# Second tile of each image's token product in three passes of rounded parts and rests

## What is computed

```python
p = x.reshape(n, C, NP, PS, NP, PS).transpose(0, 2, 4, 1, 3, 5).reshape(n, NP * NP, D_IN)
tokens = jnp.einsum('npd,hd->nph', p, W) + b
tokens = jnp.concatenate([cls, tokens], axis=1) + pos_embed[None]
...
h = jnp.concatenate([h, txt], axis=1)
h = h + _L0_attn_ref(_layernorm(h, axis=-1), L0_attn_W_qkv, L0_attn_b_qkv)
h = h + _L0_ffn_ref(_layernorm(h, axis=-1), L0_ffn_Wg, ..., L0_ffn_Wsd)
```

## Time and profile before

| | us |
|---|---|
| median of 3 runs | 701.12 |
| lowest, highest | 699.82, 701.9 |
| the profiled execution | 699.24 |
| its span in the trace | 697.4 |
| TensorE busy | 678.6 |
| VectorE busy | 469.4 |
| ScalarE busy | 332.0 |
| GpSimd busy | 201.4 |

### The profile page before, as it was taken

How to read it: one execution, slowest core, us unless ns; L and a number is a source line. 1 busy time by engine, 2 the same in 40 slices (tenths; PEclk the granted TensorE clock), 3 DMA queues, 4 the chain that set the end, 5 groups by cost and what they waited for, 6 DMA issues and landing times.

```text
span 697.4 us, 16667 instructions
## 1 busy us (share of the span) xinstructions
PE 678.6 (97%) x4613; PEld 635.5 (91%) x4614; DVE 469.4 (67%) x1490; ACT 332.0 (48%) x803; POOL 201.4 (29%) x309
## 2 busy tenths in 40 slices
PE   6989999999999999999999999999999999999997
PEld 6879988899988888799999999999999999999997
DVE  2357878888788878765666566666675757576653
ACT  2245555565555666444445343434444434343543
POOL 3022223223223210202323233333333242424240
PEclk9899999999999999999999999999999999999999
DMA  7236434545344321733445454545454545454542
GB/s 232 89 99 210 129 112 148 158 154 152 115 137 141 108 95 63 182 61 63 95 103 108 104 103 106 105 106 104 105 107 102 106 102 107 98 108 97 103 88 56
DMA packets 75188, 79.54 MB, mean 114 GB/s; under 512 B 6505, under 2 KB 67065, under 8 KB 75162
## 3 DMA queue, kind: packets, MB, share of 16 engines
q1 hardware_dynamic: 62538, 65.69, 33.9%
q0 software_dynamic: 11760, 12.31, 11.6%
q10 hardware_dynamic: 864, 1.25, 0.6%
HBM read 51.91 MB, written 19.32 MB: 102 GB/s over the span
## 4 chain that ended last, share of the span: by engine, by line
PE 80%; DVE 10%; issue 4%; ACT 2%; DVEq 1%; POOL 1%; POOLq 0%; ACTq 0%
PE bank L1275 24%; PE bank L1243 12%; PE bank L1292 8%; PE bank L1073 8%; PE bank L1255 8%; PE bank L1061 6%; PE bank L1293 4%; PE bank L1103 3%; PE bank L1217 2%; DVE stats L1454 1%; DVE w_raw L1565 1%; PE bank L1131 1%; PE bank L1088 1%; DVE y_B L1474 1%; DVE h L1490 1%
## 5 line engine op out<-in xcount | busy, mean ns | idle before, releaser
L1740 DVE TENSOR_TENSOR s_inter<-s_gate,bank 128x384 f32<-128x384 f32 (+1 forms) x112 | 60.2, 539 | 73.2 <-PE bank L1275 67.0
L906 ACT ACTIVATE s_gate<-bank 128x384 f32<-128x384 f32 (+1 forms) x112 | 53.5, 478 | 79.1 <-PE bank L1275 79.0
L1292 PE MATMUL bank<-s_dn,s_in_hi 128*128 128x384 f32 (+1 forms) x287 | 88.9, 371 | 0.3 <-DVE s_in_lo L1748 0.2
L727 POOL DMA_INDIRECT result<-y_rows,put_idx x40 | 59.8, 1496 | 57.8 <-DVE y_rows L1727 42.1
L1275 PE MATMUL bank<-all_hiA,s_hi 128*128 (+4 forms) x210 | 73.9, 352 | 0.6 <-DVE s_inter L1740 0.6
L1293 PE MATMUL bank<-s_dn,s_in_lo 128*128 128x192 f32 (+1 forms) x287 | 72.9, 254 | 0.0
L1073 PE MATMUL bank<-w_tok,patches 128*128 128x192 f32 x360 | 68.4, 343 | 4.2 <-DMA patches<-xp 4.0
L798 ACT ACTIVATE y<-h,shift,rstd 128x192 f32<-128x192 f32 (+2 forms) x96 | 45.6, 538 | 54.9 <-POOL shift L658 54.9
L1275 PE MATMUL bank<-all_B,s_lo 128*128 (+4 forms) x210 | 70.2, 334 | 0.0
L1275 PE MATMUL bank<-all_B,s_hi 128*128 (+4 forms) x210 | 70.2, 334 | 0.0
L1275 PE MATMUL bank<-all_loA,s_hi 128*128 (+4 forms) x210 | 70.0, 333 | 0.0
(11 more groups left out here) (216 smaller groups left out, 1831.5 us busy)
## 6 DMA issues: line engine op xcount, KB each, us to landing
raw_gu<-wgu SPq DMA_DIRECT2D x22, 464.0 KB, 5.4
raw_gu<-wgu SPq DMA_DIRECT2D x44, 232.0 KB, 6.0
patches<-xp SPq DMA_DIRECT2D x15, 588.0 KB, 4.3
down_w<-wdn SPq DMA_DIRECT2D x22, 348.0 KB
result<-s_rows POOLq DMA_DIRECT2D x12, 288.0 KB
result<-h SPq DMA_DIRECT2D x16, 192.0 KB
yw_rows<-y SPq DMA_DIRECT2D x16, 192.0 KB
all_hiA<-y_hiA SPq DMA_DIRECT2D x16, 162.5 KB, 2.6
```

Source lines behind the costliest of these rows:

```text
L727: pool.indirect_dma_start(acc[:, :], bass.IndirectOffsetOnAxis(ap=put_idx[:, h:h + 1], axis=0), y_rows[:, h, :], None, compute_op=ALU.add) ...
L906: act.activation(s_gate[m % 2][0:r, 0:width], up_banks(m, alone)[0][0:r, 0:width], ACT.Silu).then_inc(s_gate_ready, 1)
L1292: pe.matmul(bank[0:r, 0:2 * D], s_in_hi[:, m, rows], s_dn[:, m, :], start=m == 0, stop=False)
L1740: dve.tensor_tensor(s_inter[m % 2][0:r, 0:width], s_gate[m % 2][0:r, 0:width], up, ALU.mult).then_inc(s_inter_ready, 1)
```

## The change

The second tile of the token product of images 4 to 15 (steps 2 to 13) is computed in three passes of float32r with only 70 columns of patches, 69 of which hold patches of the image. Its operands are made so: `p_hi` (ScalarE, in each step behind `turned`) is the rounded copy of patch columns 128 to 197, `p_lo` (GpSimd, in each step behind `rstd_pool` of image n) is the rest, and `wt_hi` and `wt_lo` are the same for the weights, made once in step 1 by ScalarE and VectorE. Tile 0, and both tiles of images 0 to 3, stay as they were. Only rows 0 to 69 of the second half of the PSUM bank are written; the other rows keep the zeros of image 3.

```diff
+REST = IMG - 128 + 1
+SPLIT_FROM = 4
...
+        over_patches_1 = Region(images.at).place
         patches_1 = sb("patches_1", [128, KC, 256])
         addend_1 = sb("addend_1", [128, D])
+        p_hi = over_patches_1("p_hi", [128, KC, REST], F32R)
+        p_lo = over_patches_1("p_lo", [128, KC, REST], F32R)
+        wt_lo = over_patches_1("wt_lo", [128, KC, D], F32R)
+        wt_hi = Region(first_at).place("wt_hi", [128, KC, D], F32R)
...
+                def patch_low(n):
+                    pool.wait_ge(p_hi_ready, n - SPLIT_FROM + 1)
+                    pool.tensor_tensor(p_lo[:, :, :], patches[:, :, 128:128 + REST], p_hi[:, :, :].bitcast(F32),
+                                       ALU.subtract).then_inc(p_split, 1)
+
                 def step(n):
...
                     rstd_pool(pool, n2, n)
+                    if not isinstance(n, int) or SPLIT_FROM <= n + 2 < B:
+                        patch_low(n + 2)
                     if not isinstance(n, int) or n < B - 2:
...
+                def patch_hi(n):
+                    act.wait_ge(patch_in, 16 * n - 16)
+                    act.wait_ge(tok_mm, n)
+                    act.activation(p_hi[:, :, :], patches[:, :, 128:128 + REST], ACT.Copy).then_inc(p_hi_ready, 1)
+
+                def token_weights_hi():
+                    act.activation(wt_hi[:, :, :], w_tok[:, :, :], ACT.Copy).then_inc(wt_hi_set, 1)
...
                         turned(n + 1)
+                    if not isinstance(n, int) or SPLIT_FROM <= n + 2 < B:
+                        patch_hi(n + 2)
...
-                step(1)
+                step(1, token_weights_hi)
...
-                    for c in range(KC):
-                        mm = pe.matmul(tok_ps[:, t * D:(t + 1) * D], own[:, c, t * 128:(t + 1) * 128],
-                                       w_tok[:, c, :], start=c == 0, stop=c == KC - 1)
+                    if t == 1 and (not isinstance(n, int) or n >= SPLIT_FROM):
+                        pe.wait_ge(p_split, n - SPLIT_FROM + 1)
+                        pe.wait_ge(wt_lo_set, 1)
+                        ps = tok_ps[0:REST, D:2 * D]
+                        for c in range(KC):
+                            pe.matmul(ps, p_hi[:, c, :], wt_hi[:, c, :], start=c == 0, stop=False)
+                            pe.matmul(ps, p_hi[:, c, :], wt_lo[:, c, :], start=False, stop=False)
+                            mm = pe.matmul(ps, p_lo[:, c, :], wt_hi[:, c, :], start=False, stop=c == KC - 1)
...
+                def token_weights_lo():
+                    dve.wait_ge(wt_hi_set, 1)
+                    dve.tensor_tensor(wt_lo[:, :, :], w_tok[:, :, :], wt_hi[:, :, :].bitcast(F32), ALU.subtract).then_inc(wt_lo_set, 1)
...
-                step(1)
+                step(1, token_weights_lo)
```

More of the change, by code:

```diff
@@ L168, in build @@
         raw_sl = sb("raw_sl", [3 * LAST, D])
+        first_at = images.at
         first = sb("first", [128, FIRST])
@@ L330, in build @@
         patch_in = sem("patch_in")
+        p_hi_ready = sem("p_hi_ready")
+        p_split = sem("p_split")
+        wt_hi_set = sem("wt_hi_set")
+        wt_lo_set = sem("wt_lo_set")
         patch_1_in = sem("patch_1_in")
@@ L1071, in tokens @@
                         wait(pe, h0_ready, n)
-                    for c in range(KC):
-                        mm = pe.matmul(tok_ps[:, t * D:(t + 1) * D], own[:, c, t * 128:(t + 1) * 128],
-                                       w_tok[:, c, :], start=c == 0, stop=c == KC - 1)
+                    if t == 1 and (not isinstance(n, int) or n >= SPLIT_FROM):
[6 more added lines that the diff above has]
+                            mm = pe.matmul(ps, p_lo[:, c, :], wt_hi[:, c, :], start=False, stop=c == KC - 1)
+                    else:
+                        for c in range(KC):
+                            mm = pe.matmul(tok_ps[:, t * D:(t + 1) * D], own[:, c, t * 128:(t + 1) * 128],
+                                           w_tok[:, c, :], start=c == 0, stop=c == KC - 1)
                     if t == 1:
```

## The result

| | before | after |
|---|---|---|
| median, us | 700.95 (20 runs, taken beside those of after) | 697.42 (20 runs) |
| the profiled execution, us | 699.24 | 697.39 |
| its span, us | 697.4 | 695.5 |

The ratio is 0.9953, 95% interval 0.9939 to 0.9967: 3.3 us faster, where 702.0 was forecast and the range began at 697.6. Every part of the change lies where the prediction put it; TensorE's wait for GpSimd is a quarter of what it was costed at.

A forecast was written before the change was run, and what follows sets the result against it. TensorE was taken as the bound (97% busy). Eleven steady steps at +0.06 us (-0.34 gain, +0.40 wait) and step 2 at +0.26 summed to +0.9 us, put on the 701.12 median: 702.0 us, range 697.6 to 705.8.

The forecast's parts named there:

- 18 x 0.09 = 1.63 us, 0.34 under the 1.97: Second token product on TensorE: 18 passes of 0.09 us replace 1.97 us, the whole gain, 0.34 us per step.
- It costs nothing: ScalarE's rounding of 420 elements, under 0.970 us, fits where ScalarE has nothing to do for 2.40 us.
- The room of 0.99 us: From the end of GpSimd's shift, 202.82, to TensorE reaching the second token product, 203.81: 0.99 us for the subtraction.
- Both sides of the 0.99 us move together: GpSimd's chain starts from VectorE's, which starts when the token product ends; a shorter product hides no wait next step.
- VectorE would yield to the subtraction: VectorE's mask begins at 203.83, in the subtraction's last 0.2 us; VectorE yields, having 1.05 us idle, at no cost.
- 0.11 us per pass with 128 columns: TensorE's matmul pace with 128 columns loaded; at it the 18 passes would take 2.0 us and gain nothing.
- the wait is 0.16 + 1.05 + 0.12 + 0.06 - 0.99 = 0.40 us per step: TensorE's wait for GpSimd's subtraction: start, duration, hand-over and slower first interval, less the room, 0.40 us per step.
- rivals 1 and 2: rival 1 has its own line; rival 2: GpSimd's subtraction becomes the bound, 704.9 us or about 708, chance 0.34.
- the sign of being wrong that the prediction names first: GpSimd's subtraction off from 1.05 us by more than 0.2 us either way, since 11 steps multiply it.
- rival 1: GpSimd's subtraction takes one pass, 0.53 us, TensorE waits for nothing, the gain comes through: 697.6 us, chance 0.18.
- all steps alike: Each of the 11 steady steps was to change by -0.34 + 0.40 = +0.06 us.
- late by about 0.6 us: Step 2: VectorE's one-time weight subtraction delays y_loA and TensorE's query by about 0.6 us; the step costs +0.26.

The follow-up runs named there:

- experiment 1: Changed kernel with the twelve p_hi passes first and the six p_lo passes last, behind the wait: 694.64 us, ratio 0.9958 to the kernel before.
- experiment 2: Changed kernel making all split parts and waiting for them, but still computing the six float32 products: 698.86 us, ratio 1.0004 to the kernel before.
- experiment 8: Changed kernel without the six p_lo passes, p_lo still made and awaited before the last column of passes: 688.82 us, ratio 0.9853.
- experiments 3 and 7: experiment 3 has its own line; 7 is the changed kernel with GpSimd's text copy moved ahead of the subtraction: 701.28 us, ratio 1.0029.
- experiment 3: Changed kernel with an extra GpSimd subtraction of three slices, into a tile nobody reads, ahead of p_lo: 701.28 us, ratio 1.0038.
- experiment 4: experiment 1 with all 128 columns of patches instead of 70: 700.79 us, ratio 1.004 to the kernel before.
- Experiment 10: Changed kernel with VectorE waiting, before y_loA, until GpSimd has finished ve and below: 705.3 us, ratio 1.0064.
- experiment 11: Changed kernel with the subtraction in two halves, each with its own signal, awaited before the first and tenth passes: 697.67 us, ratio 0.995.
- third group: Four runs on one chip: experiment 1 again (697.2 us), the changed kernel again (696.85 us), Experiment 10 and experiment 11.
- experiment 5: The changed kernel run again without any edit: 695.83 us, ratio 0.9951 to the kernel before.
- first two groups: The first eight follow-up runs, four to a group, on two chips other than the third group's; expert loop iterations took 35.40 us.

## Why the prediction was wrong

*Right.* TensorE is the bound and the change touches its steps only. "18 x 0.09 = 1.63 us, 0.34 under the 1.97": 1.60 and 0.37 (experiment 1). "It costs nothing" of the rounding, the text copy and VectorE: experiment 2. The room of 0.99 us: 0.98 (shift's end 200.12, TensorE free at 201.10). "Both sides of the 0.99 us move together": experiment 8. That a cost ahead of the wait is paid in full: experiments 3 and 7. That VectorE would yield to the subtraction where the two meet: experiment 3. 0.11 us per pass with 128 columns: experiment 4.

*Wrong: the step "the wait is 0.16 + 1.05 + 0.12 + 0.06 - 0.99 = 0.40 us per step".* Its form holds, its terms were too large and all but the room on one side:

| term | forecast | measured | from |
|---|---|---|---|
| from the shift's end to the start | 0.16 | -0.03 | 200.12 to 200.09 |
| duration | 1.05 | 1.00 | p_lo, 200.09 |
| hand-over to TensorE | 0.12 | 0.06 | 201.09 to 201.15 |
| slower first interval | 0.06 | 0.05 | 0.14 instead of 0.09 |
| less the room | 0.99 | 0.98 | 201.10 - 200.12 |
| the wait | 0.40 | 0.10 | |

The start alone is 0.19 of the 0.30. I took a middle between two gaps of GpSimd's rows, 0.06 and 0.26, and neither of them came. The listing of the order has one difference: the text copy's two waits stand alone as instructions ahead of it, the subtraction's wait is part of the instruction itself. That this is the reason is not shown, for below, which has no wait at all, starts 0.06 behind ve, while in experiment 3 p_lo, without a wait of its own, starts before the recorded end of the one ahead. There were rows without a gap in the trace of before, GpSimd's memsets at its start; here the second is recorded from 0.07 us before the end of the first:

```profile
3.27 0.37 POOL L671 MEMSET y_B<- 128x326 f32 x1
3.57 0.36 POOL L672 MEMSET left<- 96x320 f32 x1
```

With the terms as measured a steady step changes by 0.10 - 0.36 = -0.26 us, and 14.44 - 14.70 is that. The duration, which I took for the great unknown and which rivals 1 and 2 were built on, was off by 0.05, so the sign of being wrong that the prediction names first, a subtraction off by more than 0.2 us, did not appear and the forecast failed all the same: rival 1's result came without its cause. Its condition, a subtraction of under 0.78 us, is not met; the gain comes through because the fixed terms are small.

The duration by the Trainium skill (GPSIMD Engine Reference, Elementwise — side-by-side cycle accounting) was an estimate of 1.07 us, and the prediction does not say how it comes about; the page's 4497 ns for 2048 elements, scaled to 420, give an estimate of 0.92. The trace has 1.01, between the two. That is near the two whole copies, one per input, that the sum took, and far from the one pass of 0.53.

*Wrong: all steps alike.* Three of eleven have room to spare and gain the full 0.36 (14.34 instead of 14.70 in step 6). The rows of before that would have told it are those of steps 6, 9 and 10, where between the shift's end and the product lie 1.63 to 1.66 us. I read one steady step (headed step 13; its product, at 203.81 us, is the tenth of the twelve, so it is step 11), and took one stretched row as a risk of the new operation instead of as a cost that was already in the 0.99. Experiment 10 showed that cost.

*Wrong: "late by about 0.6 us" in step 2.* Splitting the weights took 1.16 us on ScalarE (idle 0.92 behind it) and 1.33 on VectorE, as forecast. But it started 0.15 us earlier than I put it, counted from the operations ahead, and before y_loA VectorE had been waiting 0.42 us for ScalarE, which stands in the earlier trace rows and which I didn't take off. Only 0.12 us came out (experiment 2). The shift came later too, so the room of that step fell from 1.64 to 1.02 us and TensorE waits there as in the steady steps; its step gains 0.28, not 0.36.

Together: 8 x -0.26, 3 x -0.36 and 0.12 - 0.28 for step 2 make -3.3 us; the times say -3.3. The profiled spans differ by 1.9 only, mostly because the profile of after has the 35.6 us iterations, 9 x 0.22 = 2.0 us, and that of before has not.

*Chances.* The case that came had 0.18. Both bounds of the start were wrong on the same side: even with its lower one, 0.06, the steady step would have come to -0.04 us and the forecast to no change. A bound below it, no gap at all, was missing, and so was any lower bound of the hand-over.

## What to carry to other kernels

Where one operation stands between two engines with a microsecond of room, the fixed parts (start, hand-over) weigh as much as its duration; bound the start from all kinds of rows, those without a gap too. Give the first passes operands that are ready early and put those that come late last: it took the whole wait away in the traces, some 1.2 us, too little to show in the times of whole executions. Read the room in several steps, not in one: here it was 0.98 us in eight and 1.6 in three.

## What the runs showed of the hardware

- GpSimd starts an instruction whose wait is already met 0.03 to 0.04 us before the recorded end of the one ahead; two waits that stand alone ahead of the text copy go with 0.26 us behind the short shift and with nothing behind the long subtraction (the copy starts at 201.04, the subtraction ends at 201.09).
- A VectorE subtraction with both inputs in SBUF, when it begins first, stretches the small GpSimd operation beside it: y_loA that of ve from 0.24 to 0.45 us, y_B (197.86 in after, 0.01 ahead) that of below from 0.23 to 0.58. With the order reversed by a wait both are short (experiment 10). It cost 0.4 to 0.5 us in a chain of 5.15.
- The other way round VectorE yields. Its mask takes 0.43 us in the earlier trace rows, where GpSimd is idle; 0.54 in after (201.12), beside the text copy that began at 201.04; 0.82 in experiment 3 and 1.09 in experiment 4, where it begins while the subtraction runs and has 0.55 and 0.81 us of it ahead. The subtraction is not lengthened: 1.01 us in experiment 3, and in experiment 4 1.84 in every step, also in those where the mask meets only its last 0.2 us. When 0.14 us are left of it (experiment 11) the mask is not stretched. The Trainium skill (SBUF — State Buffer, practical consequences) says that the first to issue keeps the shared pair, which it states for VectorE's two-port modes, and that an operation like these, with two inputs in SBUF, contends with GpSimd's reads; the rows fit the rule for this case too.
- The same programs took 35.40 us per iteration of the expert loop on two chips and 35.6 on a third and in the profile of after. In the profile of after, ScalarE sits idle for 0.84 us ahead of one s_gate with nothing named as the cause, and so 8 times (6.7 us in all); in the runs of the third group 7 or 8 times; in the run of experiment 5, and in all others of the first two groups, never:

```profile
462.38 0.49 ACT L935 ACTIVATE s_gate<-bank 128x384 f32<-128x384 f32 x1 [0.84 <-issue]
```

Why is open. It is 2 us of a span, more than half of what the change is worth, so spans of profiles from different occasions were not a measure of it.
